# A Macaron block on one core: the mixture gathers its rows by slot, and the fp4 feed-forward keeps its block maxima and reciprocals in PSUM

## What is computed

```
x = x + 0.5 * ffn0(LN(x))      # fp4 feed-forward, 128 -> 352 -> 128
x = x +       attn0(LN(x))     # gated delta rule, 16 heads of 8
x = x + 0.5 * ffn0(LN(x))      # the same feed-forward again
x = x + 0.5 * moe(LN(x))       # mixture
x = x +       attn1(LN(x))     # causal attention, 16 heads of 8
x = x + 0.5 * moe(LN(x))       # the same mixture again
```

## Time and profile before

| | |
|---|---|
| median of 3 runs | 968.8 us (967.94 to 971.24) |
| profiled execution, own time | 966.31 us |
| its span | 964.6 us |
| PE busy | 747.5 us (77%) |
| DVE busy | 708.9 us (73%) |
| POOL busy | 396.8 us (41%) |
| ACT busy | 359.0 us (37%) |
| granted TensorE clock, mean | 0.918 |

### The profile page before, as it was taken

How to read it: one execution, slowest core, us unless ns; L and a number is a source line. 1 busy time by engine, 2 the same in 40 slices (tenths; PEclk the granted TensorE clock), 3 DMA queues, 4 the chain that set the end, 5 groups by cost and what they waited for, 6 DMA issues and landing times. The chain is left out here.

```text
span 964.6 us, 16498 instructions
## 1 busy us (share of the span) xinstructions
PE 747.5 (77%) x6011; PEld 498.1 (52%) x6011; DVE 708.9 (73%) x1214; ACT 359.0 (37%) x602; POOL 396.8 (41%) x586
## 2 busy tenths in 40 slices
PE   0466797777769999857687893579899999878893
PEld 0245445766669998535554562334444444354462
DVE  8999688899996879799943235599899999065232
ACT  1122382110004631112131351428788888622251
POOL 3344302888887940134506254033333333204253
PEclk9989799999998999888879996759999999998997
DMA  7100000000000000310001312655200000000313
GB/s 186 29 1 0 2 1 1 1 1 1 1 1 1 2 2 0 115 33 1 0 1 46 84 39 76 218 93 109 38 10 9 10 9 10 11 1 31 85 39 112
DMA packets 41236, 33.94 MB, mean 35 GB/s; under 512 B 6438, under 2 KB 35686, under 8 KB 41158
## 3 DMA queue, kind: packets, MB, share of 16 engines
q1 hardware_dynamic: 38022, 26.80, 11.5%
q0 software_dynamic: 2560, 5.31, 1.7%
q10 hardware_dynamic: 576, 0.79, 0.3%
HBM read 17.51 MB, written 13.80 MB: 32 GB/s over the span
## 5 line engine op out<-in xcount | busy, mean ns | idle before, releaser
L2041 DVE TENSOR_REDUCE blockmax<-c_bank 128x8 f32<-128x1024 f32 x144 | 173.2, 1219 | 22.4 <-PE c_bank L2174 18.3
L2110 ACT ACTIVATE PT<-c_bank 128x1024 f32<-128x1024 f32 x144 | 146.8, 1026 | 37.4 <-PE c_bank L2196 35.1
L2210 PE MATMUL c_bank<-PT,V 128*9 128x256 f32 (+1 forms) x1408 | 86.7, 343 | 3.7 <-ACT OT L2102 2.6
L915 PE MATMUL sums<-prod,ident 128*128 128x128 f32 x512 | 67.8, 289 | 26.7 <-DVE prod L947 26.7
L2167 PE MATMUL c_bank<-KA,QA 48*128 48x128 bf16 (+3 forms) x608 | 60.6, 284 | 23.9 <-DMA QA<-qk_parts_dram 11.8
L915 PEld LDWEIGHTS sums<-prod,ident 128*128 128x128 f32 x512 | 62.5, 200 | 31.9 <-DVE prod L947 31.8
L1991 POOL TENSOR_SCALAR_AFFINE_SELECT PT<-PT 128x256 f32<-128x256 f32 x128 | 49.1, 407 | 69.5 <-ACT PT L2110 69.3
L1676 POOL DMA_INDIRECT routed_results<-results_m,rows_m x48 | 45.9, 957 | 64.2 <-DVE results_m L1650 62.4
L1656 DVE TENSOR_TENSOR r_h_m<-r_silu_m,r_gu_m 128x256 f32<-128x256 f32 x48 | 20.2, 421 | 66.0 <-ACT r_silu_m L1641 66.0
L391 PE MATMUL gu_f<-gu_wT,xqT_f 128*128 128x352 f32 x128 | 51.0, 551 | 17.8 <-DVE h_f L311 17.8
L1390 POOL DMA_INDIRECT sorted_rows<-xs_m,where_m x32 | 30.9, 967 | 77.7 <-DVE where_m L1514 68.6
(11 more groups left out here) (342 smaller groups left out, 1790.1 us busy)
## 6 DMA issues: line engine op xcount, KB each, us to landing
sorted_rows<-blank SPq DMA_DIRECT2D x2, 1584.0 KB, 12.3
rows_m<-sorted_rows SPq DMA_DIRECT2D x12, 264.0 KB, 5.0
back_m<-routed_results SPq DMA_DIRECT2D x8, 256.0 KB, 3.7
qk_parts_dram<-qk_parts SPq DMA_DIRECT2D x8, 256.0 KB, 2.6
qk_parts_dram<-qk_parts SPq DMA_DIRECT2D x4, 384.0 KB, 2.8
QA<-qk_parts_dram SPq DMA_DIRECT2D x6, 256.0 KB, 4.6
KA<-qk_parts_dram SPq DMA_DIRECT2D x6, 256.0 KB, 7.2
m_gu<-in_rt_gate SPq DMA_DIRECT2D x1, 1024.0 KB, 6.1
```

The lines of the kernel that those rows point to most:

```text
L915: ins = nc.tensor.matmul(sums[:, kind, 0], k.ident[:, :], prod[:, kind, e // HALF, :, e % HALF, :], start=(e == 0), stop=(e == DH - 1))
L2041: nc.vector.tensor_reduce(blockmax[:, h % 2, :, HALFQ * n:HALFQ * (n + 1)], slot_of((1, m)).rearrange("p b (n c) -> p b n c", c=P), AX.X, ...
L2110: nc.scalar.activation(PT[:, u % PRING, :, :], slot_of((0, u)), ACT.Exp, scale=SCALE).then_inc(s_pt, 1)
L2210: ins = nc.tensor.matmul(O[32 * g:32 * g + DH + 1, f * P:f * P + n], V[:, b, j, h, :], PT[:, u % PRING, b, o:o + n], start=(a % len(VALUES ...
```

## The change

Feed-forward: `amax` and `inv` of both quantisers go to PSUM, into columns that the banks `y[:, 1]` (for x) and `gu[:, 1, 1]` (for h) have free. PE therefore waits for the division L175 of the pair before ahead of the last matmul of each `gate_up`, and in `project(1)` for that of x group 3. All 16 tiles are normalised ahead of the first quantisation. `gate_up(0)` and `gate(0)` stand ahead of the second group's transposes. For the last two pairs PE runs three `keep_busy` matmuls once h of all pairs is there. `pick` and `place` are made by ACT. The blank rows are gone.

Mixture: one block in place of two. The scaled rows are stored plainly by SP, and 16 ACT instructions scale them. From `spot` DVE makes, per token, which of 23 slots it is in (`in_slot`) and at which place (`in_lane`); one accumulated product of 16 small bf16 matmuls turns this round: for each slot and lane the number of the token (split in two parts, one made by ACT, one by POOL). From it come `source` and `target`, and POOL gathers each slot's rows by an indirect DMA and later scatters its results. There are 23 slots. The first two h of the shared expert stand on DVE behind `sources()`.

```diff
-SLOTS = TILES + EXPERTS
+SLOTS = TILES + EXPERTS - 1
...
-        self.amax = k.sb(f"q_amax{tag}", [P, self.nb], ctx=ctx)
+        small = spare if spare is not None else k.sb(f"q_small{tag}", [P, 2 * self.nb], ctx=ctx)[:, :]
+        self.amax, self.inv = small[:, 0:self.nb], small[:, self.nb:2 * self.nb]
...
+        qx = Quant(k, f"x{tag}", XTILES * D, ctx, y[:, 1, 2 * D:2 * D + 2 * XTILES * D // QBLOCK])
+        qh = Quant(k, f"h{tag}", W2, ctx, gu[:, 1, 1, FF:FF + 2 * W2 // QBLOCK])
...
-                ln.on_vector_apply(dve, 0, XTILES)
+                ln.on_vector_apply(dve)
                 for g in range(XG - 1):
                     quantise_x(g)
-                    ln.on_vector_apply(dve, (g + 1) * XTILES, XTILES)
...
+                            if j >= 1 and s == m == 1:
+                                pe.wait_ge(s_hdve, Quant.LINKS * (j - 1) + Quant.SCALED)
...
+                    else:
+                        pe.wait_ge(s_h, PAIRS)
+                        keep_busy(k, gu[:, 0, 0, :], 3)
                     turn_h(j)
...
             def _(pool):
-                pool.wait_ge(s_xs, 2)
-                pool.wait_ge(s_where, 1)
-                for t in range(TILES):
-                    nc.gpsimd.indirect_dma_start(out=rows_dram[:, :],
-                                                 out_offset=bass.IndirectOffsetOnAxis(ap=where[:, t:t + 1], axis=0),
-                                                 in_=xs[:, t, :], in_offset=None).then_inc(s_scattered, 16)
+                pool.wait_ge(s_slot, 1)
+                nc.gpsimd.tensor_tensor(number[:, :, 1, :], in_slot[:, :, :], wide(moe.full[:, :], [P, TILES, SLOTS]), ALU.mult
+                                        ).then_inc(s_number, 1)
+                pool.wait_ge(s_kept, 16 * NB)
+                pool.wait_ge(s_source, 1)
+                for j in range(SLOTS):
+                    nc.gpsimd.indirect_dma_start(out=rows[:, j, :], out_offset=None, in_=rows_dram[:, :],
+                                                 in_offset=bass.IndirectOffsetOnAxis(ap=source[:, j:j + 1], axis=0)).then_inc(s_rows[j], 16)
...
+                def token_numbers():
+                    pe.wait_ge(s_number, 2)
+                    for t in range(TILES):
+                        pe.wait_ge(s_lane, t // GROUP + 1)
+                        ins = nc.tensor.matmul(numbers, in_lane[:, t, :], number[:, t].rearrange("p a s -> p (a s)"),
+                                               start=(t == 0), stop=(t == TILES - 1))
+                    ins.then_inc(s_found, 1)
...
-                gate_up(0, 0)
+                shared_product(0, 0, 0)
                 count()
-                gate_up(0, 1)
-                for c in range(NB):
-                    down(c)
-                    if c + 1 < NB:
-                        for half in range(HALVES):
-                            gate_up(c + 1, half)
-                keep_busy(k, logits[:, :], 2)
+                shared_product(0, 0, 1).then_inc(s_sgu, 1)
+                shared_gate_up(0, 1)
+                keep_busy(k, shared_y[:, 0, :], 2)
+                token_numbers()
+                for c in range(NB - 1):
+                    shared_gate_up(c + 1, 0)
+                    shared_project(c)
+                    shared_gate_up(c + 1, 1)
...
                 chosen_expert()
-                scaled_rows()
                 sorted_place()
+                slot_and_lane()
+                sources()
```

More of the change, by code:

```diff
@@ L236, in on_vector @@
         ch.link(ins)
[L237 removed]
+        self.delta.on_vector(dve)
         dve.wait_ge(self.s_w, 5 * 16)
@@ L1370, in moe_front @@
-        (s_ndve, s_tp, s_xT, s_lg, s_top, s_score, s_hot, s_cnt, s_dve, s_xs, s_where, s_scattered, s_gu, s_silu, s_h, s_y,
-         s_res) = (k.sem(f"{n}{tag}") for n in names)
+        which = f("which", [P, SLOTS], I32)
+        low, high, whole = f("low", [P, TILES]), f("high", [P, TILES]), f("whole", [P, TILES], I32)
+        in_slot = f("in_slot", [P, TILES, SLOTS])
+        number = f("number", [P, TILES, 2, SLOTS], BF16)
+        in_lane = f("in_lane", [P, TILES, P], BF16)
+        filled, vacant = f("filled", [P, SLOTS]), f("vacant", [P, SLOTS])
@@ new lines, in moe_ffn @@
+        source, target = f("source", [P, SLOTS], I32), f("target", [P, SLOTS], I32)
+        rows, results = f("rows", [P, SLOTS, D]), f("results", [P, SLOTS, D])
+        rowsT, silu, h, hT = f("rowsT", [P, 2, P]), f("r_silu", [P, 2, INNER]), f("r_h", [P, 2, INNER]), f("r_hT", [P, 2, INNER])
+        back = f("back", [P, TILES, D])
+        bank = k.ps(f"m_bank{tag}", [P, 8, BANK], ctx=ctx)
+        shared_gu = bank[:, 0:4, :].rearrange("p (h m) c -> p h m c", m=2)
+        shared_y = bank[:, 4:6, :]
@@ new lines, in _ @@
+                sp.wait_ge(s_stored, 16 * SLOTS)
+                for g in range(4):
+                    sp.dma_start(back[:, 4 * g:4 * g + 4, :], tiled(result_dram[0:TOKENS, :])[:, 4 * g:4 * g + 4, :]).then_inc(s_back[g], 16)
+                if out is not None:
+                    for g in range(4):
+                        sp.wait_ge(s_added, g + 1)
+                        sp.dma_start(out.rearrange("b (t p) c -> p (b t) c", p=P)[:, 4 * g:4 * g + 4, :], k.x[:, 4 * g:4 * g + 4, :]
+                                     ).then_inc(s_out, 16)
+                    sp.wait_ge(s_out, 4 * 16)
@@ L1412, in count @@
                     for n, to in enumerate((moe.not_yet, moe.ones)):
-                        ins = nc.tensor.matmul(counts[:, n, 0:TILES * EXPERTS], to[:, :], hot, start=True, stop=True)
+                        ins = nc.tensor.matmul(counts[:, n * BANK // 2:n * BANK // 2 + TILES * EXPERTS], to[:, :], hot, start=True, stop=True)
                     ins.then_inc(s_cnt, 1)
-                def gate_up(c, half):
+                def token_numbers():
[5 more added lines that the diff above has]
+                    ins.then_inc(s_found, 1)
```

395 lines of the change are left out of this document (188 added, 207 removed).

## The result

The changed kernel took 937.3 us (median of 4, 932.35 to 937.78), the kernel before, run beside it, 968.4 (967.62 to 971.24). The ratio is 0.965, with a 95% interval of 0.962 to 0.968: 31 us faster. The forecast was 937.5. The execution shown here took 937.06 us, its span is 935.3: 29.3 us less than the span before.

The account below looks back on a forecast made before the run. DVE, held by POOL, bounds the feed-forwards; a chain of waiting engines bounds the mixtures. Feed-forwards -21.1 and mixtures -10.2 give -31.3: from 966.3 to 935.0, plus 2.5 to the median, 937.5 us; range 926 to 950.

Parts of the forecast that it names:

- DVE's removed time: Feed-forwards: PSUM operands for L173 and L175, normalisation first, pick and place on ACT remove 26.6 us of DVE time.
- rival (a): Feed-forwards: PSUM does not free DVE, L173, L175 or L176 stays held; 11 us back, 948.5; chance 0.12.
- PSUM operands at no price: Feed-forward DVE: 96 instructions with PSUM operands cost 0.4 us, written as 0; the skill page's figures would give 6.2.
- Rival (c): Feed-forward DVE: writing a maximum or reciprocal to PSUM is dear, at most 8.6 us, 946; chance 0.04.
- Holds of L176: Feed-forward DVE: L176, SBUF-only, now meets POOL on x groups; 2.1 us per stage, 4.2 come back.
- PE late in the feed-forwards: Feed-forwards: h waits for gate_up products behind PE's idle time; about 5 us come back.
- rival (e): Feed-forwards: PE holds its clock after the gaps and h never waits; 5 us more gained, 932.5; chance 0.14.
- The new wait of gate_up: Feed-forward PE: gate_up's last matmul waits for the division; taken as 0, at worst 0.5 a pair, 8 in all.
- The stages' ends: Feed-forward ends: added matmuls let the last transposes and projection run at 2.4 GHz; 1.3 us gained a stage.
- Mixtures, -5.1 each: Mixtures: earlier first routed product, bound by the shared expert, not the gathers, and one slot less; -5.1 us each.
- the case at 1.2 GHz: Mixtures: PE fallen to 1.2 GHz after its gap, for the first products; first routed product at 534.7, not 533.0.
- rival (d): Mixtures: gathers do not overlap, one every 3.3 us; each mixture 13 us longer, 974 in all, slower; chance 0.03.

Follow-up runs that it names:

- e5: Changed kernel with feed-forward mostly as before (SBUF amax/inv, four normalisation groups, old PE and ACT order, no products ahead of the last two pairs): 997.7 us, ratio 1.012.
- e1: Changed kernel with amax and inv of both quantisers back in SBUF, without PE's two waits for the division: 949.1 us, ratio 0.975.
- e2: Kernel before with only amax and inv in PSUM and PE's two waits for the division: 955.3 us, ratio 0.986.
- e7: Changed kernel with unread products in PE's idle times, including three ending delta attention's first block: 963.8 us, ratio 0.981, second chip.
- e6: Changed kernel without the three unread products ahead of the transposes of the last two pairs: 976.6 us, ratio 0.992, second chip.
- e3: Changed kernel with the sixteen tiles normalised in four groups again, one ahead of each quantisation: 943.7 us, ratio 0.970.
- e12: Changed kernel with unread products in PE's idle times, two ahead of the last pair, shared expert's first two h between in_lane groups: 965.6 us, ratio 0.985.
- e4: Changed kernel with three more unread products at the end of delta attention's first block: 932.6 us, ratio 0.960.
- e9: Changed kernel itself, unaltered, run again on the second chip: 972.1 us, ratio 0.989 to the kernel before.
- e10: Kernel before, unaltered, run again on the second chip for a profile: 982.3 us, one run.
- e11: Changed kernel with GpSimd waiting after six gathers until all h of the shared expert are there: 977.3 us, one run, second chip.

## Why the prediction was right, and where it was not

- **DVE's removed time, 26.6 us: right.** L173 on h gave 16 x 0.587 = 9.4 (forecast 9.8), L173 and L175 on x 1.9 and 1.8 as forecast, the normalisation 19.8 - 8.4 = 11.4 (10.9). L175 on h had been held a little too (971 to 886 ns: 1.4), which I left out. `pick` and `place`, 2.2 by the forecast, gave 1.5 in e5. e1 and e2 show the PSUM part from both sides, 10.6 us and 13.2, or 10.5 without the faster ends, and so rival (a) was wrong.
- **PSUM operands at no price: right.** L172 and L174 on h are 8 ns longer each, which over the 48 instructions that write to PSUM makes 0.3 us. By the Trainium skill, "VectorE: DVE Perf Modes", section on the TRN2 errata, my estimate had been 6.2 us for the 96 instructions; the rows after don't bear it out. Rival (c) fell with the 8 ns.
- **Holds of L176, 4.2: right** (8 x 0.454 = 3.6).
- **PE late in the feed-forwards, 5: too small.** h waited 7.5 us. In feed-forward 1 the reckoning held (h(0) 2.4 against 1.8, h(3) and h(4) 0.35 together). In feed-forward 2 h(1) waited 3.6, not 1.3, since the forecast had taken gate_up(1) at 2.4 GHz and it ran at 1.2 behind a gap of 3.3 us, and h(3) 1.0. In e7, with PE kept at work, both gate_up run at 2.4 GHz, h waits 1.0 us in that stage instead of 4.65, and the stage is 4.0 us shorter: it was the clock. This is rival (e), which the change as it stands did not get.
- **The new wait of gate_up, 0: right.** Pairs come every 5.73 us, 5.75 us in e2, which has the wait too. PE does wait for the division, 0.45 us at gate_up(2), but h is no later for it.
- **The stages' ends, 1.3 each: the size was off, and the cause is only half shown.** The last projection is fast as forecast (1.60), but six instructions end 1.4 us behind POOL, not 0.8. e6 gives 0.8 to 1.0 in feed-forward 2. That the fast projection needs the three products is true of the changed kernel by e6, but not in general: e2 has it without them.
- **Mixtures, -5.1 each: too small.** The shared expert bound, not the gathers, as forecast: in the timeline PE goes from the second chunk to the first routed product with gaps of no more than 1.2 us, all of them for DVE's h, and the rows of the first slots are there before it. To the first routed product it was 42.8 us in mixture 1 (forecast 44.3) and 45.7 in mixture 2 (46.0, the case at 1.2 GHz). The slow clock behind the token numbers came in both (3.66 and 3.78 us for four products); in mixture 2 it lasted through the next projection too (2.88 us, 2.00 in mixture 1). What the forecast lacked is the stage's start: the eight `keep_busy` instructions took 3.67 us in mixture 1, where they had taken 5.86 before, and 6.32 in mixture 2 (5.37 before). In e1 and e3 they took 5.37, and mixture 1 was 99.2 us and not 97.4. That the products at the end of feed-forward 2 give this start isn't shown, since e2 has none and starts in 3.67, and e7 has them and needs 6.67. From the first routed product to the last scatter it was 42.6 us instead of 45.0: one slot, 1.7, and 0.8 that I had missed, since the first two slots' transposes are now done before.
- **Not in the forecast at all:** that an untouched stage can move by 4 us by its clock, and that the mixture with gathers gains on one chip and loses on another. The total was hit only because the mixtures' surplus stood against delta attention's loss. On the second chip the ratio was 0.989, about 10 us, and 937.5 out of reach; rival (d), gathers that bind, had the right sign for the mixtures there (+8.5 us together), but not the mechanism: the gathers came on time, and the other engines stood still.

## What to carry to other kernels

An operand moved to PSUM takes a VectorE instruction out of GpSimd's way at no measurable price, and one small operand is enough; look then for the next instruction with SBUF alone. When a chain gets shorter, look whether the time saved comes back as waiting for a product that stands behind a gap of PE, and at what clock that product ran: unread products in the gaps were worth 4 us in a stage where the 5 us that normalising first saves on DVE had given 0.8. And compare kernels with indirect DMAs on more than one chip before believing a gain of a few per cent, and stage by stage rather than by their totals.

## What the runs showed of the hardware that was not expected

- Delta attention, the same instructions in every kernel, took 290.1 to 299.0 us. The same gap of 3.1 us was followed by a granted clock of 1.00 in one execution and 0.50 in another; before the gap PE did the same eight products of 5.40 us in both.
- On the chip of e5 to e12, and not on that of e1 to e4, ACT stood still in mixture 1 for 9.4 us (e9) to 14.3 us (e12) and DVE for 15.1 to 17.9, from the midst of 23 gathers to some 4 us behind the last, while GpSimd's issues kept coming every 1.25 us. With 16 scatters (e10) the standstills were shorter. The records of e6, e9, e11 and e12 have no packet of an instruction queue in these standstills. The mixtures of the changed kernel took 33.9 us more there (231.8 - 197.9), those of the kernel before 10.8 (223.3 - 212.5).
- ACT made 128x128 tiles from SBUF with a scale every 0.30 us (16 in 4.78), about the pace of DVE's normalised ones (0.28 by the earlier trace rows).
